# First token group's start chain rebuilt, and the second group's third tile projected in the first group's down stage

## The reference, cut to what matters

```python
# x: (2, 2048, 1024), that is 4096 tokens of 1024 numbers
xn = layernorm(x)                                   # over the last axis
f = rfft(xn); corr = irfft(f * conj(f), n=1024)     # autocorrelation of each token
weights, delay = top_k(corr, 6)                     # int(log(1024)) = 6
s = sum(roll(xn, delay_k) * softmax(weights)_k)     # agg
def qlora(x, wq, A, B): return x @ tile(wq, (1, 4)).T + (x @ A.T @ B.T) * 0.5
g = silu(qlora(silu(qlora(xn, w1q, a1, b1)) * qlora(xn, w3q, a3, b3), w2q, a2, b2))
out = x + s * g                                     # hidden size 2752, rank 2
```

## Time and profile before

| | |
|---|---|
| time, median of 3 runs | 903.14 us (902.80 to 903.35) |
| the profiled execution's own time | 903.65 us |
| its span, first to last instruction | 901.9 us |
| mean granted TensorE clock | 0.975 |
| PE busy | 848.8 us, 94% of the span |
| DVE busy | 649.8 us, 72% |
| ACT, POOL busy | 299.1 us, 304.6 us |

### The profile page before, as it was taken

The page is one execution under the profiler, slowest core; times in us unless marked ns, Lnnn a source line. Parts: engine busy times, 40 slices in busy tenths (PEclk is TensorE's granted clock), DMA queues, the critical chain, the costliest instruction groups (busy, mean ns, idle before and its releaser), DMA issues.

```text
span 901.9 us, 11119 instructions
## 1 busy us (share of the span) xinstructions
PE 848.8 (94%) x4042; PEld 437.6 (49%) x4042; DVE 649.8 (72%) x1007; ACT 299.1 (33%) x441; POOL 304.6 (34%) x394
## 2 busy tenths in 40 slices
PE   3769779799999999999999999999999999999996
PEld 2323226543466344844466344844466344844465
DVE  7587897578966888677966788667976878643534
ACT  4653334133232333133332333233332333223231
POOL 5462392343430455044430455043430445100000
PEclk9898988899999999999999999999999999999999
DMA  9816010621125011431125011431124110330003
GB/s 314 233 42 229 7 29 1 170 94 36 31 54 186 27 34 50 127 117 36 30 53 183 28 36 36 130 129 36 30 53 160 51 36 7 95 122 0 1 1 141
DMA packets 53719, 71.53 MB, mean 79 GB/s; under 512 B 37152, under 2 KB 39424, under 8 KB 53392
## 3 DMA queue, kind: packets, MB, share of 16 engines
q1 hardware_dynamic: 53648, 70.69, 25.7%
HBM read 45.51 MB, written 16.78 MB: 69 GB/s over the span
## 4 chain that ended last, share of the span: by engine, by line
PE 79%; DVE 11%; ACT 3%; DVEq 3%; issue 3%; POOL 0%; DMA 0%; SPq 0%; ACTq 0%
PE g L1065 22%; PE u L1065 20%; PE zb L1144 5%; PE g L1168 5%; PE u L1168 5%; PE u L1177 4%; PE u L1175 4%; PE g L1177 4%; PE g L1175 4%; PE g L1082 3%; DVE junk L680 2%; DVEq L741 2%; DVE h L725 1%; DVE acc L737 1%; ACT w_abs L508 1%
## 5 line engine op out<-in xcount | busy, mean ns | idle before, releaser
L508 ACT ACTIVATE sil<-g,winv 128x512 f32<-128x512 f32 (+1 forms) x176 | 120.0, 683 | 280.2 <-PE g L1082 237.6
L1065 PE MATMUL g<-xt,w_h 128*128 128x512 f16 x672 | 204.2, 386 | 8.7 <-DVE w_l L911 5.5
L1065 PE MATMUL u<-xt,w_h 128*128 128x512 f16 x672 | 202.7, 384 | 0.0
L725 DVE SCALAR_TENSOR_TENSOR h<-u,winv,sil 128x512 f32<-128x512 f32 x168 | 125.7, 748 | 98.2 <-ACT sil L508 83.5
L680 DVE CUSTOM_DVE_ANT_0 junk<-xn,abc 128x1024 bf16<-128x1024 f32 x112 | 160.1, 1430 | 6.4 <-issue 2.2
L438 POOL TENSOR_TENSOR ve<-mv,three 128x1 f32<-128x1 f32 x32 | 6.8, 212 | 366.8 <-DVE mv L663 366.8
L1065 PE MATMUL g<-xt,w_l 128*128 128x512 f16 x336 | 129.2, 384 | 0.0
L1065 PE MATMUL u<-xt,w_l 128*128 128x512 f16 x336 | 128.6, 383 | 0.0
L1065 PEld LDWEIGHTS u<-xt,w_h 128*128 128x128 f16 x672 | 66.5, 99 | 81.5 <-issue 3.9
L1065 PEld LDWEIGHTS g<-xt,w_h 128*128 128x128 f16 x672 | 57.3, 98 | 96.7 <-issue 37.8
L859 DVE SCALAR_TENSOR_TENSOR ob<-xr,c_mean,gg 128x1024 f32<-128x1024 f32 x32 | 41.1, 1283 | 76.4 <-ACT gg L508 50.6
(11 more groups left out here) (165 smaller groups left out, 1189.0 us busy)
## 6 DMA issues: line engine op xcount, KB each, us to landing
xr<-in_x SPq DMA_DIRECT2D x34, 512.0 KB, 4.7
out_x<-ob SPq DMA_DIRECT2D x32, 512.0 KB, 2.9
xf<-in_x SPq DMA_DIRECT2D x30, 512.0 KB, 3.7
raw_w<-in_w2t SPq DMA_DIRECT2D x1, 2560.0 KB
raw_w<-in_w1t SPq DMA_DIRECT2D x3, 768.0 KB, 8.1
raw_w<-in_w3t SPq DMA_DIRECT2D x3, 768.0 KB, 9.6
abc<-in_a SPq DMA_DIRECT2D x1, 2048.0 KB, 13.4
xt<-hl SPq DMA_TRANSPOSE x32, 3.2
```

The lines of the kernel that those rows point to most:

```text
L508: return nc.scalar.activation(out, in_, f, **kw)
L725: stt(out=h[0:n, p % NH, :], in0=up, scalar=winv[0:n, 2 * (p // 6) + 1:2 * (p // 6) + 2], in1=sil[0:n, p % 2, :], op0=ALU.mult, op1=ALU.mu ...
L1065: o = mm(bank[:], a, x, start=opens and t == 0, stop=closes and t == len(terms) - 1)
```

## The change

The first group's start chain and its share of weight preparation are laid out anew:

- Tiles 0 and 1 of x are loaded into `xrs`, and stay there raw, so the later reload of them is gone. Raw x is transposed on PE; the mean is taken out of A instead (`a_raw` centred on DVE), the reciprocal root multiplies the projected result (`rsb`, `zc`), and the 32-column matmuls of `z0` are summed over four strips by one matmul with `sel`.
- The raw tiles are folded to quarters (`fold`, two on POOL, two on DVE), ACT normalises the 256 columns (`quarter_normal`), PE transposes them (`quarter_across`), and ACT and DVE copy them out of PSUM as high and low part (`xt_high`, `xt_low`). The DMA transposes of `xt` and the `sums`/`quarters` of the first group go. POOL makes the differences of raw tiles (`raw_differences`).
- Loads: ACT issues `low` and the ten loads of B; SP loads block 0 of the weights between the x tiles, and `abc` only after the first two tiles of the second group.
- BLOCK is (0, 4, 10, 16, 22). The bound is a sum of squares over all rows by a matmul with ones (`scale_sum`), which needs no maximum and transpose. B is split once for block 0 and once for the rest, on DVE (`b_step`), and scaled by ACT in bf16 (`b_scale`). PE runs the chains of pair 1 before `lora(0, 1)`.
- In the first up stage, DVE's statistics, projections and the weight steps stand on other p; only tiles 0 and 1 of the second group are projected there. `last_projections(1)` takes tiles 2 and 3. `w2_tail` is one instruction; part of it goes to POOL (`w2_low(5)`), and POOL makes the `w2_low` in three portions.

The diff, cut to its core:

```diff
-BLOCK = (0, 6, 12, 18, NP_)
+BLOCK = (0, 4, 10, 16, NP_)
...
-        STATS_AT, NORM_AT = (1, 7, 13, 19), (2, 8, 14, 20)
-        Z_AT = {3 + 6 * q + r: (q, r) for q in range(3) for r in range(4)}
-        C_AT, I_AT, FLAG_AT = (5, 9), (11, 15), 18
+        STATS_AT = [(2, 8, 14, 19)] + [(1, 7, 13, 19)] * (NG - 1)
+        NORM_AT = [(3, 9, 15)] + [(2, 8, 14, 20)] * (NG - 1)
+        Z_AT = [{(4 if i == 0 else 3) + 6 * q + r: (q, r) for q in range(2 if i == 0 else 3) for r in range(4)} for i in range(NG)]
...
-        LOW_AT = {5 * b + k - 4: (b, k) for b in range(1, NB) for k in range(5)}
-        HIGH_AT = {0: 1, 4: 2, 9: 3}
+        BOUND_AT = {3: ((2, 0),), 4: ((2, 1),), 5: ((3, 0), (3, 1))}
+        HIGH_AT = {1: ((1, 0), (1, 1)), 6: ((2, 0), (2, 1)), 10: ((3, 0),), 11: ((3, 1),)}
+        LOW_AT = {1: ((1, 0, 0), (1, 0, 1)), 2: ((1, 1, 0), (1, 1, 1)),
+                  7: ((2, 0, 0), (2, 0, 1)), 8: ((2, 1, 0), (2, 1, 1)),
+                  11: ((3, 0, 0),), 12: ((3, 0, 1),), 13: ((3, 1, 0),), 14: ((3, 1, 1),)}
+        B_AT = {3: 1, 8: 2, 12: 3}
...
# SP
-            for q in range(4):
-                front_load(0, q)
...
+            front_load(0, 0)
+            front_load(0, 1)
+            block_load(0, 0)
+            front_load(0, 2)
+            block_load(0, 1)
+            front_load(0, 3)
+            sp.dma_start(sel[:], d["sel"]).then_inc(sel_loaded, 16)
...
+            front_load(1, 0)
+            front_load(1, 1)
             sp.dma_start(abc[:].rearrange("p r c -> p (r c)"),
...
-            for q in (2, 0, 3, 1):
-                xt_load(0, q)
...
# POOL
+            def raw_differences(q):
...
+                tt(yh[:], x[:, 0:HALF], x[:, HALF:L], ALU.subtract).then_inc(raw_diff, 1)
...
+                nc.gpsimd.tensor_scalar(yh[:], yh[:], rs[:, q:q + 1], None, ALU.mult).then_inc(diff_done, 1)
...
+                tt(out[:, 1:DQ], yh[:, 1:DQ], yh[:, HALF - 1:DQ:-1], ALU.subtract).then_inc(ab_done, 1)
+                tt(out[:, DQ + 1:HALF], yh[:, 1:DQ], yh[:, HALF - 1:DQ:-1], ALU.add).then_inc(ab_done, 1)
...
                 for q in range(4):
-                    if q == 3:
-                        for n in range(HN if i == 0 else 0):
-                            w2_low(n)
+                    if i == 0 and q == 2:
+                        w2_low(0)
+                        w2_low(1)
+                    if i + 1 < NG:
+                        spread(i + 1, q)
+                    if i == 0 and q == 2:
+                        w2_low(2)
+                    if i == 0 and q == 3:
+                        for n in range(3, HN + 1):
                             w2_low(n)
# ACT
-            for q in range(4):
-                normalise(0, q)
-            w_bound(0)
...
+            w_bound(0, 0)
+            for k in range(4):
+                x_copy(0, k)
+            w_bound(0, 1)
+            for q in range(3):
+                quarter_normal(q)
+            x_copy(1, 0)
+            x_copy(1, 1)
+            quarter_normal(3)
+            b_cast(0, 0)
+            act.wait_ge(rsb_ready, 1)
+            A(rsb[:], mb[:], ACT.Copy).then_inc(rsb_done, 1)
+            xt_high(0)
+            xt_high(1)
+            w_high(0, 0)
+            w_high(0, 1)
+            b_cast(0, 1)
+            w_bound(1, 0)
...
+            w_bound(1, 1)
...
+            b_scale(0)
+            b_cast(1, 0)
# DVE
             def last_projections(i):
-                for r in range(4):
-                    project(i, 3, r)
+                for q in range(2 if i == 1 else 3, 4):
+                    for r in range(4):
+                        project(i, q, r)
...
-                tt(w2_l[0:64, n, :], raw_w2[0:64, n, :], w2_h[0:64, n, :].bitcast(F32), ALU.subtract)
-                nc.vector.memset(w2_l[64:P, HN, :].bitcast(F32), 0.0)
...
+                stt(out=w2_l[64:P, HN, :], in0=b2_hi[64:P, :].bitcast(F32), scalar=low[64:P, 3:4], in1=raw_b2[64:P, :],
+                    op0=ALU.mult, op1=ALU.add).then_inc(w2t_done, 1)
...
-            for q in range(4):
+            for q in range(3):
                 stats(0, q)
-            quarters(2)
-            quarters(3)
-            x_copy(7)
-            w_tops(0, 2)
-            x_copy(1)
-            w_scale(0, 2)
+            fold(2)
+            stats(0, 3)
+            drain()
+            fold(3)
+            w_scale(0, 1, mb[:, 0:3])
+            x_copy(2)
             x_copy(3)
-            x_copy(5)
-            b_scale(0)
+            b_step(0, 0)
+            xt_low(0)
+            xt_low(1)
+            dve.wait_ge(rsb_done, 1)
+            dve.wait_ge(z0_ready, 1)
+            tt(zc[:], zb[:], rsb[:], ALU.mult).then_inc(zc_done, 1)
             for m in range(2):
                 for k in range(2):
                     w_low(0, m, k)
-                b_split(0, m)
+            b_step(0, 1)
...
+            b_step(1, 0)
+            w_scale(1, 1, zb[:, 0:3])
...
                     if p:
                         add_chunk(i, p - 1)
...
+                    if i == 0:
+                        for b, m, k in LOW_AT.get(p, ()):
+                            w_low(b, m, k)
+                        if p == 3:
+                            b_step(1, 1)
...
+                    if i == 0 and p == 5:
+                        w_scale(2, 2, mb[:, 0:6])
# PE
+                elif i == 0 and p == 1:
+                    chain(gb[1], 0, 1, True, False)
+                    chain(ub[1], 1, 1, True, False)
+                    scale_sum(1, zb, 0)
+                    lora(0, 1)
...
+            def z0(half):
+                t = slice(256 * half, 256 * half + 256)
+                for k in range(8):
+                    s = 32 * (k % 4)
+                    o = mm(zb[s:s + 32, t], aT[:, k, :], xT[:, k, t], start=k < 4, stop=k >= 4)
```

More of the change, by code:

```diff
@@ L46, with block_of @@
 HALF_ROWS = P // 2
+def block_of(p):
+    return max(b for b in range(NB) if BLOCK[b] <= p)
 def pair_rows(p):
@@ L566, in down, with w_bound @@
                     A(gg[:, 512 * half:512 * half + 512], bank[:], ACT.Silu).then_inc(dn_read, 1)
[L568 removed]
+            def w_bound(b, m):
                 lo, hi = block_cols(b)
[L570 to L574 removed]
+                act.wait_ge(w_loaded[b][m], 16)
+                if b or m:
+                    act.wait_ge(wsum_done, 2 * b + m)
+                with nc.allow_low_precision(reason="a bound with a margin"):
+                    A(w_sq[:, :, 0:hi - lo], raw_w[b][:, m], ACT.Square,
@@ L596, in w2_high, with xt_high @@
+            def xt_high(k):
+                act.wait_ge(xq_ready, 1)
+                A(xt[:, k, :], xq_banks[k][:], ACT.Copy).then_inc(xth_done, 1)
             def w2_high(n):
@@ L624, in _ @@
                     gate(i, p)
-                    if i == 0 and p in HIGH_AT:
-                        w_high(HIGH_AT[p])
-                    if i == 0 and p in LOW_AT and LOW_AT[p][1] in (0, 2):
-                        b_high(LOW_AT[p][0], LOW_AT[p][1] // 2)
-                    if i == 0 and p in W2_AT:
-                        w2_high(W2_AT[p])
-                    if p in C_AT:
-                        square(i, C_AT.index(p))
-                    if not last and p in NORM_AT[:3 if i == 0 else 4]:
-                        normalise(i + 1, NORM_AT.index(p))
+                    if i == 0:
+                        for b, m in HIGH_AT.get(p, ()):
+                            w_high(b, m)
+                        if p == 2:
+                            b_cast(1, 1)
+                        if p in B_AT:
+                            b_scale(B_AT[p])
+                        for b, m in BOUND_AT.get(p, ()):
+                            w_bound(b, m)
+                        if p in W2_AT:
+                            w2_high(W2_AT[p])
+                    if p in C_AT[i]:
+                        square(i, C_AT[i].index(p))
+                    if not last and p in NORM_AT[i]:
+                        normalise(i + 1, NORM_AT[i].index(p))
                     if p % 4 == 1 and p > 1:
@@ new lines, in _ @@
+            pe.wait_ge(dev_done, 12)
+            pe.wait_ge(wall_read, 1)
+            for q in range(4):
+                o = nc.tensor.transpose(mb[:, q * P:(q + 1) * P], rs[:, q:q + 1].broadcast_to([P, P]), ident[:])
+            o.then_inc(rsb_ready, 1)
+            quarter_across(3)
+            pe.wait_ge(xa_done, 6)
+            pe.wait_ge(xd_done, 2)
+            z0(1)
+            pe.wait_ge(zc_done, 1)
+            pe.wait_ge(sel_loaded, 16)
+            mm(mb[:], sel[:], zc[:], start=True, stop=True).then_inc(z0_ready, 1)
```

559 lines of the change are left out of this document (279 added, 280 removed).

## The result

The changed kernel takes 887.6 us (median of 4 runs, 886.57 to 888.29), the kernel before 903.0 beside it (4 runs): a ratio of 0.982, 95% interval 0.981 to 0.984. Timed again beside the last three experiments it took 887.3 against 902.8, a ratio of 0.983 (0.981 to 0.984). The profiled execution is the one of 886.57 us, 17.1 less than the 903.65 before.

A forecast was written before the change was run, and what follows sets the result against it. Only the start of the second group's first matmul matters, set mainly by DVE's queue ahead of it. 903.65 - 13.0 - 12.0 + 1.7 = 880.3, forecast 880 us; own range 873 to 887, with rivals 868 to 890.

The forecast's parts named there:

- rival B: Start chain does not shorten, first product at 42: 887, or 890 with the up stage at 83; chance 0.13.
- Term 1: Start to the first product: from 48.26 to about 35.3 us, gain 13.0.
- the x tile at 14.3: Start chain: the last x tile's statistics on DVE begin at 14.3 us, against 10.77 before.
- Term 2: First to last product in the first up stage: from 92.2 to about 80 us, gain 12.
- PE's wait at pair 16: First up stage: PE waits 1 to 3 us there for `w_low`.
- The four projections taken out of the stage: First up stage: 4 of 12 projections leave DVE's queue at 1.62 each, 6.5 us less work.
- Term 3: Last product to `zs`: from 30.3 to about 32 us, loss 1.7.
- `w2_low(3)` to `w2_low(5)` beside DVE's tail sums: Tail before `zs`: contention of between 0 and 4 us, taken as made up by the clean first half.
- A: First up stage no longer bound by DVE, PE reaches its 68 us plus two stalls: 868; chance 0.17.
- C: Lower clock through the whole first up stage because PE's waits are cut into many short ones: 927; chance 0.02.
- D: Tail eats what the up stage gives, leaving 3.5 us of the start and losing 1.7: 902; chance 0.02.
- three signs of failure: Last x tile's statistics after 17; DVE idle between products under 6 or over 16; no PE wait at the transposes.

The follow-up runs named there:

- the last three experiments: Combinations on the changed kernel: e4 with e5, then e2 added, then the move of e1 added; 881.6, 879.8 and 878.0 us.
- e4: Changed kernel, with B's loads issued by SP behind the x tiles and `sel` instead of by ACT from the beginning; 885.5 us, ratio 0.980.
- e7: Changed kernel, with POOL's raw differences of the first group waiting for the four `w_low` of the first block; 889.0 us, ratio 0.984.
- e5: Changed kernel, with `w2_low(0)` and `w2_low(1)` moved behind the root of the second group's third tile, ahead of its differences; 883.9 us, ratio 0.977.
- e2: Changed kernel, with the second group's third tile projected in the first up stage again; 883.7 us, ratio 0.978.
- e1: Changed kernel, with `w2_low(3)` to `w2_low(5)` put ahead of the root of the second group's fourth tile on POOL; 886.6 us, ratio 0.982.
- e8: Changed kernel with the edits of e1 and e2 together; 883.3 us, ratio 0.977.
- e3: Kernel before, with only the projection of the second group's tile 2 moved to the first group's down stage; 902.8 us, ratio 1.000.
- e10: Changed kernel with the edits of e4, e5 and e2 together; 879.8 us, ratio 0.9743.

## Why the prediction was right, and where it was not

880 was forecast, 887.6 measured: inside the range, but 0.6 above the 873 to 887 that the forecast has for its own case, and within rival B's time. The direction and the place were right: everything is decided by the second group's first matmul, and what follows it is unchanged. The gain in the profiled execution is 17.1 where the sum has 23.3. The three terms are short by 1.7, 1.5 and 3.9; 0.9 from the transposes on, which the sum has at nothing, goes the other way.

**Term 1, -13.0 predicted, -11.3 measured** (-11.1 by the fifth product, in both profiles). The first chain was put at 26.5 and came at 27.34 and 26.09. The step that failed is the x tile at 14.3: it came at 15.98 and 16.40, 1.7 and 2.1 late. The steps from there to the first chain took less than their 12.2, 11.4 and 9.7, and those from the chain to the product more than their 8.8, 9.6 and 9.1. The price of B, 3.2, was nearly right, and e4 shows that it is paid ahead of x (2.4 and 2.9 against the two profiles); what I had taken off for a DVE that is late anyway was not to be taken off. Contention was given 2 us in all; 1.45 of it is in the four `w_low` alone (e7).

**Term 2, -12 predicted, -10.5 measured** (81.8 us; 83.0 in the second profile). DVE's queue does carry this stage. Its work came out at 67.1 us, below the 68.8 (its items add up to 68.3), its idle time at 14.7 instead of 11. The step that failed is PE's wait at pair 16: put at 1 to 3 us, it is 7.55 (6.7 in the second profile), because two `w2_low` fall exactly beside the `w_low` and the projection ahead of it. I had entered the two that moved out as 1.5 us saved and the three that stayed as costing their average. e5 shows that two of them cost 4.2 where they stand: 2.2 of DVE's work and 2.0 of its idle time (4.15 to 2.12). What made the other 1.7 us of idle time too many is not shown. The four projections taken out of the stage, entered at their full 6.5, brought only 1.8 to 2.5 (e2): the rest turned into waiting. The 1.62 for each was itself a mean over unlike places: in the kernel before these four had taken 2.2.

**Term 3, +1.7 predicted, +5.6 measured.** The step that failed is "`w2_low(3)` to `w2_low(5)` beside DVE's tail sums: between 0 and 4", of which I took nothing, as made up by the clean first half. They stretch three instructions by 5.8 us and cost the way to `zs` 4.6 (e1; 4.7 in e8 against e2), above the upper bound too; the rest of the tail came out 0.7 below its sum. The row for it stood among mine, an `hf_l` of 2.81 beside `w2_low`; three `w2_low` meet three such instructions and stretch them by 1.6, 2.2 and 2.1. The Trainium skill, "SBUF — State Buffer", Who interferes with whom, says that the read interface which DVE's second input shares with POOL is held exclusively, so that one waits for the other's whole instruction. The rows agree: a `w2_low` alone takes 2.35 us on POOL, the second and third here 2.81 and 2.84, and DVE's 2.84 and 2.77 beside them last as long.

**The rivals.** B's time (887 to 890) is what came, but its mechanism is not: the first chain was put at 33 in it, and came at 27. A (868) fails at term 2; PE waits 11.3 us for `w_low`. C did not come: the clock is 0.92 in the first up stage. D was right about one part and wrong about the whole: moving the third tile down brings nothing in the kernel before (e3), and costs 3.6 to 4 us in the changed one (e2). The gain comes from the rest, the earlier start and a shorter up stage. Which of the many steps of the new start chain brought its 11 us is not shown: only B's loads (e4) and the raw differences (e7) were moved one by one.

None of the three signs of failure came: the statistics began ahead of 17, DVE's idle time lay between 6 and 16, and PE did wait at the transposes. The largest error, 3.9 us in term 3, had no sign of its own. That the time lies in the range is in part luck: its upper end was there for B, whose reason was another. What would have made the number right was in the rows: the contention piece by piece, which the prediction names as its weakest step.

## What to carry to other kernels

When two engines contend for SBUF, don't price the contention as an average: list which instruction of the bound engine stands beside each of the other's, because one that holds a wait of PE costs all of it and one that stands ahead of idle time costs little or nothing (e5 against e1). List again after every move: in e10 the moved `w2_low` stands beside a projection that e5 hadn't there. Work moved out of a stage is worth its full duration only as long as the queue there has no idle time; ahead of a single last result, as `zs` here, it costs all of it. Loads that are issued on another engine "beside" the first input can hold it back all the same (e4: 2 to 3 us). And work that is put late on a helper's queue delays what stands behind it there, as the root in e7.

## What the runs showed of the hardware

**The clock comes back at different times after the same wait.** In two profiles of the same changed kernel PE waits 11.23 and 11.20 us for `zs` and then runs the same matmuls. In the first the sixth of 512 columns is the last that takes longer than 0.40:

```profile
157.22 0.63 PE L1246 MATMUL g<-w_h,hf_l 128*128 128x512 f32 x1
157.65 0.46 PE L1246 MATMUL u<-w_h,hf_l 128*128 128x512 f32 x1
157.95 0.39 PE L1237 MATMUL g<-w_h,hf_h 128*128 128x512 f32 x1
```

In the second it is the twelfth:

```profile
159.17 0.63 PE L1246 MATMUL g<-w_h,hf_l 128*128 128x512 f32 x1
159.60 0.57 PE L1246 MATMUL u<-w_h,hf_l 128*128 128x512 f32 x1
160.00 0.40 PE L1237 MATMUL g<-w_h,hf_h 128*128 128x512 f32 x1
```

Ahead of the transposes the granted clock was 0.5 in both; from 158 to 162 us it is 1.00 in the first and 0.75 in the second (0.63 us for a matmul is the level of 1.2 GHz, 0.39 that of 2.4), with PE busy without a gap in both. From the transposes to the second group it is 9.89 us in one and 11.15 in the other. So 1.3 us of a difference between two single profiles can be the clock alone. e5's profile has 10.9 for this stretch, which is one reason why its second group gains less than its median; the profiled execution, 884.90, is also the slowest of its five.

**Small DMA issues hold their engine.** In the profile of e2, as in the changed kernel, ACT issues ten loads of B one after the other before its first instruction:

```profile
1.16 5.08 ACTq L674 DMA_DIRECT2D raw_b<-in_b  x8
6.27 1.10 ACTq L677 DMA_DIRECT2D raw_b<-in_b  x2
7.40 1.28 ACT L550 ACT_TABLE_LOAD   x1 [7.40 <-issue]
10.38 1.06 ACT L550 ACTIVATE w_sq<-raw_w 128x1024 bf16<-128x1024 f32 x1 [1.70 <-DMA raw_w<-in_w1t]
```

That is 0.55 to 0.64 us for each, and ACT runs nothing until 7.40. Here it holds nothing up: ACT's first work on data, at 10.38, has waited 1.70 us more for a load of weights (1.92 in the changed kernel). So what e4 gains comes from the transfers and not from ACT's time.
